# VectorE's first MLP round written out ahead of its loop, with its own list of MLP parts

## The reference, cut to what matters

```python
# block 1: layer norm, modulated per sequence; 16 query heads of 32 on 4 key heads; windowed mask
h = (x - mu) * rsqrt(var + eps) * (1 + scale) + shift
q = rope(h @ Wq.T);  c = h @ Wkd.T;  k = rope(c @ Wku.T);  v = c @ Wvu.T
x = x + softmax(mask(q @ k.T / sqrt(32))) @ v @ Wo.T
# block 2: RMS norm, modulated; 8 query heads of 64 on one key head; no mask; gated MLP of 2048
h = rms(x) * w1 * (1 + t @ tw1.T)
x = x + softmax(rope(h @ Wq.T) @ rope(h @ Wk.T).T / 8) @ (h @ Wv.T) @ Wo.T
h = rms(x) * w2 * (1 + t @ tw2.T)
x = x + (silu(h @ Wg.T) * (h @ Wu.T)) @ Wd.T
```

## Time and profile before

| | before |
|---|---|
| median of three runs | 1760.81 us |
| profiled execution, its span | 1759.8 us, 1758.0 us |
| PE busy | 1703.3 us (97%) |
| VectorE busy | 1148.6 us (65%) |
| ACT busy | 943.9 us (54%) |
| POOL busy | 407.1 us (23%) |
| share of the chain that ended last on PE | 82% |

### The profile page before, as it was taken

The page is one execution under the profiler, slowest core; times in us unless marked ns, Lnnn a source line. Parts: engine busy times, 40 slices in busy tenths (PEclk is TensorE's granted clock), DMA queues, the critical chain, the costliest instruction groups (busy, mean ns, idle before and its releaser), DMA issues.

```text
span 1758.0 us, 37788 instructions
## 1 busy us (share of the span) xinstructions
PE 1703.3 (97%) x12440; PEld 929.4 (53%) x12440; DVE 1148.6 (65%) x2850; ACT 943.9 (54%) x2769; POOL 407.1 (23%) x569
## 2 busy tenths in 40 slices
PE   6777999999999999999999999999999999999999
PEld 3445545555555545565455555555455554556444
DVE  6757675766768568675677767686576866767320
ACT  3936475453855447364674547555484645735320
POOL 3648694111211011011110212110120111102120
PEclk9797999999999999999999999999999999999999
DMA  8966599454866359472793548753584717935310
GB/s 257 166 189 115 159 249 218 92 83 115 194 142 114 76 138 194 96 129 67 175 190 79 91 118 174 163 104 85 123 199 97 139 59 168 198 79 97 115 60 25
DMA packets 527228, 234.24 MB, mean 133 GB/s; under 512 B 476336, under 2 KB 493744, under 8 KB 527024
## 3 DMA queue, kind: packets, MB, share of 16 engines
q1 hardware_dynamic: 511472, 175.09, 49.9%
q10 hardware_dynamic: 15552, 56.63, 10.3%
HBM read 90.09 MB, written 16.78 MB: 61 GB/s over the span
## 4 chain that ended last, share of the span: by engine, by line
PE 82%; DMA 3%; DVE 1%; issue 1%; ACT 0%; SPq 0%; DVEq 0%; ACTq 0%
PE up L1522 9%; PE up L1523 9%; PE up L1524 9%; PE gate L1522 9%; PE gate L1523 9%; PE gate L1524 9%; PE y L1524 4%; PE y L1523 4%; PE y L1522 4%; PE bank L1522 4%; PE bank L1524 4%; PE bank L1523 4%; PE bank L1549 2%; DMA prob_t<-prob 2%; PE bank L1593 2%; PE bank L1557 1%
## 5 line engine op out<-in xcount | busy, mean ns | idle before, releaser
L907 ACT ACTIVATE bank<-bank,low 128x128 f32<-128x128 f32 (+2 forms) x768 | 302.5, 395 | 66.6 <-DVE low L1164 36.9
L731 POOL TENSOR_TENSOR inner_t<-inner,inner_t 128x512 f16<-128x512 f32 x128 | 150.9, 1179 | 637.4 <-ACT inner_t L1103 637.3
L1171 DVE TENSOR_TENSOR prob<-bank,prob 128x512 f16<-128x512 f32 (+1 forms) x304 | 192.7, 634 | 42.9 <-ACT prob L916 41.6
L916 ACT ACTIVATE prob<-bank 128x512 f16<-128x512 f32 (+1 forms) x304 | 169.5, 558 | 59.1 <-DMA prob_t<-prob 41.1
L1477 DVE SCALAR_TENSOR_TENSOR silu<-silu,gate 128x512 f32<-128x512 f32 x128 | 87.9, 687 | 167.7 <-ACT silu L1097 166.6
L1522 PE MATMUL gate<-mlp,ring 128*128 128x512 f16 x512 | 193.9, 379 | 2.1 <-DVE silu L1477 1.2
L1522 PE MATMUL up<-mlp,ring 128*128 128x512 f16 x512 | 193.8, 379 | 0.6 <-DVE inner L1487 0.6
L1524 PE MATMUL gate<-mlp,ring 128*128 128x512 f16 x512 | 194.0, 379 | 0.0
L1523 PE MATMUL gate<-mlp,ring 128*128 128x512 f16 x512 | 193.9, 379 | 0.0
L1524 PE MATMUL up<-mlp,ring 128*128 128x512 f16 x512 | 193.9, 379 | 0.0
L1523 PE MATMUL up<-mlp,ring 128*128 128x512 f16 x512 | 193.9, 379 | 0.0
(11 more groups left out here) (183 smaller groups left out, 4050.5 us busy)
## 6 DMA issues: line engine op xcount, KB each, us to landing
ring<-wgu_dram ACTq DMA_DIRECT2D x108, 512.0 KB, 3.9
x_in<-x_dram SPq DMA_DIRECT2D x18, 512.0 KB, 3.8
x_res<-x_mid SPq DMA_DIRECT2D x16, 512.0 KB, 3.0
wgu_dram<-ring SPq DMA_DIRECT2D x16, 512.0 KB, 3.5
out_dram<-x_res SPq DMA_DIRECT2D x32, 256.0 KB, 2.3
inner_t<-wd_t_dram SPq DMA_DIRECT2D x4, 1024.0 KB, 9.5
ring<-wg_t_dram SPq DMA_DIRECT2D x16, 256.0 KB, 4.2
ring<-wu_t_dram SPq DMA_DIRECT2D x16, 256.0 KB, 4.6
```

The source lines that it names most:

```text
L731: pool.tensor_tensor(inner_t[:, 1, f, :], inner[:], inner_t[:, 0, f, :], ALU.subtract).then_inc(inner_low, 1)
L907: ins = act.activation(bank_[:, at:at + wid], bank_[:, at:at + wid], ACT.Exp, bias=low[:, j % BANKS, k:k + 1], scale=-1.0, accum_out=total)
L916: act.activation(terms(prob_place(n, g)[:, 0, :], layer, j), terms(work_bank[USE[f"unit{layer}", j] % BANKS][:], layer, j), ACT.Copy).then ...
L1171: dve.tensor_tensor(terms(place[:, 1, :], layer, j), terms(work_bank[USE[name] % BANKS][:], layer, j), terms(place[:, 0, :], layer, j), AL ...
```

## The change

VectorE's loop runs one round fewer, and the round that it loses stands ahead of it in Python, with the index (None, 1) for attention and (None, 0) for the MLP. Nothing else is edited.

```diff
             layer0((None, 0), None)
             layer1((None, 0), None)
-            with dve.Fori(0, NP - 1) as i:
-                layer0((i, 1), (i, 0))
-                layer1((i, 1), (i, 0))
+            layer0((None, 1), (None, 0))
+            layer1((None, 1), (None, 0))
+            with dve.Fori(0, NP - 2) as i:
+                layer0((i, 2), (i, 1))
+                layer1((i, 2), (i, 1))
```

## The result

The changed kernel takes 1764.16 us (median of 20 runs, 1760.67 to 1767.48) where the kernel before, run beside it, takes 1761.84 (20 runs, 1759.13 to 1764.86). The ratio is 1.0012, 95% interval 1.0006 to 1.0017: 1.1 to 3.0 us slower, where 0.9 faster was forecast. It is within 0.2%, as forecast, and beyond the top of the range, 1762.0.

A forecast was written before the change was run, and what follows sets the result against it. PE alone bounds the later rounds; only the first MLP round's 8.3 us idle can be won. From -1.15 at 290 us and -0.78 at the down product, 0.2 to 1.1 remained; 0.9 taken: 1760.81 - 0.9 = 1759.9 us, range 1758.5 to 1762.0.

The forecast's parts named there:

- The stalls go: First MLP round, `gates` of chunks 4 and 15: PE's waits for `silu`, 1.31 and 0.72 us, disappear.
- `inners` of chunk 4 keeps 0.3 us in hand: After the delayed rotary adds, `inners` ends at 224.4 and PE needs its bank at 224.84: 0.3 us spare.
- the port costs 0.1, at most 0.84: VectorE's moved adds beside POOL share an SBUF port: PE loses 0.1 us, or 0.84 if held one whole instruction.
- POOL caps the shift at 1.15, which holds to 290 us: POOL's last L790 of chunk 8 ends at 238.56, so PE comes 1.15 us earlier, kept to about 290 us.
- The second place ends at -0.78: At `gates` of chunk 15, PE's down product starts at about 293.07 instead of 293.85, 0.78 us earlier.
- prob 20 held up: `prob_lows(20)` waits behind the tanh and `gates` of chunk 15 and starts 1.09 us later.
- the stall of 0.72: PE's wait for `silu` before chunk 15's down product, 0.72 us, goes.
- its wait grows from 0.88 to about 1.9: PE's scores of unit 23 wait longer for `prob` (L1171): about 1.9 us instead of 0.88.
- The peeled round counts 0: Writing VectorE's first round ahead of its loop gains and costs 0; a bared fetch could cost up to 2.4 us.
- the wait of "up" for "inner": Sign of a wrong forecast: PE newly waits for `inners` of chunk 4 near 224.8; no size given.
- a gap of "issue": Sign of a wrong forecast: VectorE shows an issue gap in the written-out round; no size given.
- The slower rival: SP's transposing queue paces the round, the first gain is lost and unit 20 lands up to 0.95 later: 1761.7 us, 13%.

The follow-up runs named there:

- the first move alone: Kernel before with VectorE's first round written out and only `gates` of chunk 4 moved, ahead of `rope_adds`: 1763.57 us, ratio 1.0005.
- both padded kernels: Already satisfied waits put ahead of VectorE's loop, 206 in the changed kernel and 306 in the kernel before: 1773.55 and 1774.42 us, ratios 1.0066 and 1.0072.
- delay20: Written-out round without moved gates, plus VectorE waiting for chunk 15's tanh and reading 512 columns ahead of `prob_lows(20)`: 1763.41 us, 1.0005 to the kernel before.

## Why the prediction was wrong, step by step

- *The stalls go, VectorE's two gates run behind their tanhs.* Right: 1.32 us at chunk 5 (1.31 forecast), and the wait at the down product is gone.
- *`inners` of chunk 4 keeps 0.3 us in hand; the port costs 0.1, at most 0.84.* The size was off: PE waits 0.39 us and stands 0.56 later there, inside the bound. The adds took 2.46 and 2.00 us, not the 1.70 and 1.28 of before; and L1293, 2.11 and not 2.88. The neighbour was another, too: POOL's L790 ends 0.36 us after the adds start, and what runs beside them is L731 and L773, then L786. The port's rule agrees in kind; that the port and nothing else stretched them was not tried.
- *POOL caps the shift at 1.15, which holds to 290 us.* This failed. I looked at POOL's chunk 8 and not at chunk 9, whose load stands in SP's queue behind the query's turn; the turn now comes on the heels of a chunk's load and holds the queue for 6.84 us and not 4.71. The shift was gone by 248 us, 42 us ahead of where the second move needed it: in the trace a loss of 0.78 stands there in place of a gain of 1.15. By the medians the first move alone lies between 1.1 us faster and 2.6 slower.
- *The second place ends at -0.78.* **The step that failed, and the one whose price the medians show** (1.0015 alone, where no move at all has 1.0000). Its terms were near: prob 20 held up (1.09 forecast; PE stands 1.48 later there), the stall of 0.72 gone. The term that was missing is what PE does behind a long wait: half clock, about 1.6 us. From 110 to 130 us of the round the change loses 2.16 us where the forecast had a loss of 0.37. My own row of the end, "its wait grows from 0.88 to about 1.9", described TensorE idle for longer than anywhere else in this round, and I took its price for its length alone.
- *The peeled round counts 0.* Right in time (1.0000 without moves). That VectorE's loop would carry a gap of 0.37 us was not foreseen; it costs nothing that shows.
- *What would show it.* Two of the signs named as wrong came: the wait of "up" for "inner" (0.39 us), and a gap of "issue", though in the loop and not in the written-out round.
- *The slower rival* (1761.7, at 13%) had the right course. It needed a shift under 0.95 at 290 us, and there was none. Against the 1760.81 that it stood on, it gave +0.9 where +2.1 was measured, for want of the clock.

## What to carry to other kernels

Count a wait on TensorE by what the granted clock does behind it and not by its length alone: here a move that takes away one stall and lengthens another lost 2.16 us where the two lengths gave 0.37. Whether the clock falls was not to be told from the wait's length alone; it is read from the rows. A gain ahead of a shared DMA queue has to be followed through the next few transfers, since an earlier transfer meets other company there. And when code is put ahead of a loop, look at the loop's rounds for gaps of "issue": TensorE paid 1.5 to 2.1 us a round for 48 matmuls more ahead of its loop, and got most of it back when there were 128.

## What the runs showed of the hardware that was not expected

- A loop's place in its engine's instruction stream can open a gap in every round: 0.37 us on VectorE, without an effect that shows, 0.4 to 1.0 us on TensorE in kernels that lose 1.5 to 2.1 us a round. The Trainium skill (Runtime: NRT & Kernel Launch, "Instruction fetch mechanics") has instructions fetched in blocks of 256 and calls the crossing mostly hidden. VectorE's gap came and went as shifts modulo 256 would have it in both padded kernels; one instruction more ahead of the loop, in delay20, took it away too. On TensorE it was not hidden. That block borders are the cause is the reading that fits; no run looked at the fetches.
- A satisfied wait is not free: 206 of them, 103 instructions, held VectorE for 10.3 us, 0.10 us an instruction.
- TensorE's clock fell behind waits of 1.61 to 2.43 us for another engine or a DMA, in a kernel that keeps it busy 97% of the time, and stayed behind others of up to 1.70 us.
- One DMA turn of the same bytes held its queue between 4.5 and 7.4 us; it was the longer the closer it stood behind a load (0.16 to 0.18, 1.0 or 2.0 us).
